# Moving the key weights by two 64-byte lines against the other matmul operands, with narrower warm-up matmuls

## The reference

```python
q = jnp.einsum('bchw,dc->bdhw', x, theta_w) + theta_b       # 256 channels, 1024 pixels
xpool = _maxpool2(x)                                        # 16 by 16 pixels
k = jnp.einsum('bchw,dc->bdhw', xpool, phi_w) + phi_b       # 256 by 256
v = jnp.einsum('bchw,dc->bdhw', xpool, g_w) + g_b           # 256 by 256
p = jax.nn.softmax(jnp.einsum('bdn,bdm->bnm', q, k) * hp ** (-0.5), axis=-1)
vp = jnp.einsum('bdm,bnm->bdn', v, p)
out = jnp.einsum('bdhw,cd->bchw', vp, z_w) + z_b + x
```

## The kernel before

| class | function | stationary | moving | matmuls |
|---|---|---|---|---|
| queries | `project_q` | `theta` | `x_split` | 96 a half |
| keys | `project_k` | `phi` | `xp` | 48 an image |
| values | `project_v` | `xp` | `g` | 48 an image |
| scores | `scores` | `q` | `k` | 24 a half |
| attention | `attend` | `vt` | `pt` | 24 a half |
| output | `project_out` | `z` | `att` | 84 a half |

## Time and profile before

### The profile page before, as it was taken

How to read it: one execution, slowest core, us unless ns; L and a number is a source line. 1 busy time by engine, 2 the same in 40 slices (tenths; PEclk the granted TensorE clock), 3 DMA queues, 4 the chain that set the end, 5 groups by cost and what they waited for, 6 DMA issues and landing times.

```text
span 2040.4 us, 48999 instructions
## 1 busy us (share of the span) xinstructions
PE 2026.8 (99%) x17790; PEld 2024.5 (99%) x17790; DVE 1558.1 (76%) x2625; ACT 1300.0 (64%) x2228; POOL 1366.5 (67%) x828
## 2 busy tenths in 40 slices
PE   9999999999999999999999999999999999999998
PEld 9999999999999999999999999999999999999998
DVE  8878777787777877777877778777787777787777
ACT  6666666666566665666666666666666566666663
POOL 4577666776666766667766677666677666776663
PEclk9999999999999999999999999999999999999999
DMA  7565656746556565566565664656656556656554
GB/s 243 191 212 184 213 169 214 236 170 210 175 207 232 180 210 185 186 226 210 181 212 171 215 237 169 209 177 207 232 180 210 184 187 226 209 182 214 170 193 166
DMA packets 213963, 407.27 MB, mean 200 GB/s; under 512 B 12720, under 2 KB 17840, under 8 KB 213936
## 3 DMA queue, kind: packets, MB, share of 16 engines
q1 hardware_dynamic: 213792, 406.90, 59.0%
q10 hardware_dynamic: 144, 0.01, 0.0%
HBM read 272.64 MB, written 134.22 MB: 199 GB/s over the span
## 4 chain that ended last, share of the span: by engine, by line
PE 97%; DVE 2%; POOL 0%; DMA 0%; issue 0%; ACT 0%; SPq 0%; DVEq 0%; POOLq 0%
PE bank L967 97%; DVE x_top L755 0%; DVE pt_raw L736 0%; DMA x<-x 0%; DVE x_bot L755 0%; DVE pooled L708 0%; POOL att_lo L631 0%; POOL x_split_lo L613 0%; POOL att_f L626 0%; DVE x L755 0%; PE bank L974 0%; SPq L265 0%; DVE q_lo L714 0%; ACT att_hi L425 0%; DVE xp_lo L851 0%
## 5 line engine op out<-in xcount | busy, mean ns | idle before, releaser
L613 POOL TENSOR_TENSOR x_split_lo<-x,x_split_hi 128x1024 fp32r<-128x1024 f32 x255 | 614.6, 2417 | 248.4 <-ACT x_split_hi L386 226.7
L967 PE MATMUL bank<-x_split_hi,theta_hi 128*128 128x256 f32 x2048 | 565.8, 276 | 3.1 <-POOL x_split_lo L613 2.0
L967 PE MATMUL bank<-x_split_lo,theta_hi 128*128 128x256 f32 x2048 | 565.7, 276 | 0.0
L967 PE MATMUL bank<-x_split_hi,theta_lo 128*128 128x256 f32 x2048 | 565.7, 276 | 0.0
L967 PE MATMUL bank<-att_hi,z_hi 128*128 128x256 f32 x1792 | 495.4, 276 | 3.6 <-DVE x_bot L755 2.5
L967 PE MATMUL bank<-att_hi,z_lo 128*128 128x256 f32 x1792 | 494.9, 276 | 0.0
L967 PE MATMUL bank<-att_lo,z_hi 128*128 128x256 f32 x1792 | 494.9, 276 | 0.0
L736 DVE STREAM_TRANSPOSE pt_raw<-probs 32x256 f32<-32x256 f32 x1024 | 445.9, 435 | 18.4 <-ACT probs L489 1.8
L631 POOL TENSOR_TENSOR att_lo<-att_f,att_hi 128x768 fp32r<-128x768 f32 x191 | 282.6, 1487 | 159.4 <-ACT att_hi L425 159.4
L967 PEld LDWEIGHTS bank<-x_split_hi,theta_hi 128*128 128x128 f32 x2048 | 384.6, 188 | 3.5 <-issue 3.5
L967 PEld LDWEIGHTS bank<-x_split_hi,theta_lo 128*128 128x128 f32 x2048 | 384.6, 188 | 0.0
(11 more groups left out here) (76 smaller groups left out, 4390.0 us busy)
## 6 DMA issues: line engine op xcount, KB each, us to landing
x<-x SPq DMA_DIRECT2D x258, 512.0 KB, 3.9
x_top<-x SPq DMA_DIRECT2D x128, 512.0 KB, 7.0
out<-x_top SPq DMA_DIRECT2D x128, 512.0 KB, 3.3
x_bot<-x SPq DMA_DIRECT2D x126, 512.0 KB, 5.2
out<-x_bot SPq DMA_DIRECT2D x126, 512.0 KB, 6.6
x_top<-theta_wt SPq DMA_DIRECT2D x4, 256.0 KB, 5.4
x_top<-g_wt SPq DMA_DIRECT2D x4, 256.0 KB, 5.4
x_bot<-z_wt SPq DMA_DIRECT2D x4, 256.0 KB, 6.2
```

The source lines that it names most:

```text
L613: nc.gpsimd.tensor_tensor(flat(lo), flat(x_chunk(s, c)), raw(flat(hi)), ALU.subtract).then_inc(x_ready, 1)
L967: last = nc.tensor.matmul(dst, stationary(a), moving(b), start=start and n == 0, stop=stop and n == len(PRODUCTS) - 1, skip_group_check=re ...
```

## The change

The pad ahead of `att` is gone and the pad ahead of `phi` is 48 words, not 16. All operands except `phi` move down by 64 bytes; `phi` and the float32 tiles behind it move up by 64 bytes. So the operand pairs of five classes keep their distance, moving minus stationary: line 3 minus line 0 before, line 2 minus line 7 after, which is 192 bytes modulo 512 both times. For the keys (`xp` moving, `phi` stationary) it was line 0 minus line 1, 448 bytes modulo 512, and is line 7 minus line 2, 320 bytes. The warm-up tile has 160 columns, not 192, and the four stretches have 62, 29, 17 and 43 matmuls, not 52, 24, 14 and 36.

```diff
-STILL = 192
+STILL = 160
@@
-        sb("pad_a", [P, 16], f32)
         att = [sb(f"att_{s}", [P, 7, HB], f32r) for s in ("hi", "lo")]
@@
         xp = [sb(f"xp_{s}", [P, KT, M], f32r) for s in ("hi", "lo")]
-        sb("pad_c", [P, 16], f32)
+        sb("pad_c", [P, 48], f32)
         phi = [sb(f"phi_{s}", [P, KT, D], f32r) for s in ("hi", "lo")]
@@
             pe.wait_ge(still_ready, 1)
-            keep_busy(o_x[1], 52)
+            keep_busy(o_x[1], 62)
@@
             project_q(0, 1, 1)
-            keep_busy(o_x[1], 24)
+            keep_busy(o_x[1], 29)
@@
                 pe.wait_ge(exp_done, upto(turn, s, NT, NT))
-                keep_busy(o_y[0], 36)
+                keep_busy(o_y[0], 43)
@@
                         pe.wait_ge(o_added, upto(turn, s - 1, SUMS, 2 * C11 + 2))
-                        keep_busy(o_y[1], 14)
+                        keep_busy(o_y[1], 17)
```

## The result

The changed kernel takes 2074.07 us (median of 4 runs, 2072.24 to 2075.73), the kernel before 2044.0 beside it: the ratio is 1.0148 [1.0136, 1.0160], 30 us slower. The forecast was 2043.6, with a range of 2034 to 2051; the measured time lies 23 us above that range.

A forecast was written before the change was run, and what follows sets the result against it. PE was taken as the bound, time being number of matmuls times distance between starts. Terms 0 + 0.03 + 0 on a 2040.4 us span, with the median 3.2 us above it, gave 2043.6 us, range 2034 to 2051.

The forecast's parts named there:

- What bounds the kernel: Whole run: PE busy 99% of 2040.4 us, nothing feeds it late; time is number of matmuls times distance between starts.
- the slow distance: Between matmul starts on PE: 117.7 ns against 113.3 ns fast; a stretch keeps the distance at which it started.
- the first term of the sum: Queries, scores, values, attention and output: 15324 matmuls keep 192 bytes modulo 512 between operands, so 0 us.
- The keys' own term: Keys' matmuls, operand difference 448 to 320 bytes: stay at 117.7 ns, no change, between ends of -7.3 and +6.6 us.
- The second rival: Keys leave the attention slow, so all 15324 other matmuls cost 4.4 ns more: +67 us, 2111, or 2104 with fast keys; chance 0.15.
- The first rival: Keys run fast and the rest too: -7.3 us, 2036.3, or 2034.3 with the first image fast as well; chance 0.33.
- handed on: At the first attention matmul behind the keys: attention takes over slow running, +67 us; chance 0.15.
- The third rival: Keys' matmuls get a longer distance, up to 122.1 ns: up to 2050 us; chance 0.10, of which 0.08 beyond the bound.
- The place of `phi` does nothing: Key weights' address has no effect, by the skill's rule of two independent read ports: 2043.6 us, counted with the forecast.
- Five other classes: All classes but keys: moving by one line to other absolute places is no reason for a cost, 0 us.
- Warm-up: Four warm-up stretches with narrower, more numerous matmuls: +0.03 us by columns, +0.65 us as the other end.
- Start, POOL: First image's and last step's starting distance: nothing, between -2.0 and +0.2 us; POOL's float32 tiles on another line: nothing.

## Why the prediction was wrong

**What bounds the kernel** was right: PE is the bound, nothing feeds it late, and the time is number times distance. The bound of the slow distance was right as well, 4.4 ns a matmul (117.8 - 113.4).

**The step that failed** is the first term of the sum, "I cost 15324 matmuls (16764 less 30 times 48 keys) at nothing". In 15 images the 504 matmuls behind the keys ran slow, and that cost 33.6 us. The keys' own term, "I take 117.7, no change", measured -3.2 us. Both rested on "The reason is the first image: ... whoever comes from another pair into it, or out of it, falls out of step". With the keys' pair (0, 3) in place of (0, 1), a fast output leads to fast keys (5.44 us at 1930.93), which it didn't before, and fast keys lead to a slow attention, with no wait behind it in the loop to end it.

**The second rival** had the mechanism, and the run that moves `phi` alone shows it to be the cause. Its price was wrong, 2104 with fast keys, because of "since all passes are alike". They aren't: in the loop, how the keys leave depends on how they came in. Fast keys leave slow, slow keys leave fast, slow output leads to slow keys and fast output to fast keys, and so every second image is slow: 30 us, not 60.

**The chance** was wrong by a row that stood in the forecast. The one case before in which keys ran fast, the first image, is followed by slow queries. The first rival, 0.33 for fast keys with the rest fast, needed a step from fast keys into a fast stretch, which no row shows and no run has shown since: wherever keys on line 0 ran fast and a class with its moving operand on line 3 followed directly, that class was slow. Keys fast should have carried "handed on" with it.

**The third rival**, up to 122 ns in the keys, didn't come at this place; at others the keys have 119.8 and 118.8.

**The place of `phi` does nothing**: it does, by 1.4%. The rule of the Trainium skill, "TensorE: Matmul & The Clock Gate", "Part 2: What happens when you issue a matmul", of two independent read ports, isn't enough to tell the time of a matmul here: with instructions and order alike, only an address has moved. The 188 and 192 ns that the forecast set against this rule don't differ by stretch: both rows are loads of the keys, 192 for one load in three.

**Five other classes**: that their own move by one line costs nothing was right by the run with `phi` alone (2073.28 against 2074.07). That the measure is bytes modulo 512 was a guess of the front part's table, and the run with line 5 agrees with modulo 256.

**Warm-up**: +0.03 us with +0.65 as the other end. Alone it gave +3 us (0.6 to 4.9), so by that run the end was too near, though nothing of it lies in the loop of its profile. Two other pairs of kernels with the narrow and the wide warm-up lie closer: the changed kernel and the one with `phi` alone, 30.1 and 29.3 us above before; `vt` on line 2 and on line 6, 3.3 and 3.8 us below. So the size isn't settled, nor where it arises.

**Start, POOL**: 1.6 us more ahead of the chain, 0.4 behind it, in one profile each; POOL's busy time went from 1366.5 to 1363.7 us. Neither changes the picture. Two small slips of the forecast's sums (31 x 0.24 is 7.4, not 7.3; 4.4 ns x 1488 is 6.5 us, not 6.6) don't either.

What stays open is why a step keeps or turns the distance. I had a theory of it, moments of a 6.67 ns beat at which the moving operand's line lets a matmul start; it missed with `xp` on line 3, with `phi` on line 0, with the added warm-up matmul and, by the attention, with `vt` on line 2, and the last two expectations rest on steps seen before, not on it. Neither the beat nor the five cycles that an expectation gave a step are shown by any run. The steps themselves are shown, in every image of the loop in which they occur but for one case (moving line, stationary line, modulo four; a dash where none occurs):

| step | coming in fast | coming in slow |
|---|---|---|
| output (3, 0) to keys (0, 1) | slow | slow (once, with `phi` on line 5) |
| output (3, 0) to keys (0, 3) | fast | slow |
| keys (0, 1) to attention (3, 0) | - (to queries slow, in the first image) | fast |
| keys (0, 3) to attention (3, 0) | slow | fast |
| keys (0, 0) or (0, 2), 119 to 120 ns, to attention (3, 0) | - | fast |
| keys (0, 3) to attention (3, 2) | slow | - |
| attention (3, 2) to scores (3, 0) | fast | fast (slow once, behind a warm-up) |
| attention (3, 0) to scores (3, 2) | fast | slow |
| scores (3, 2) to values (3, 0) | - (to queries fast) | fast |
| between equal pairs (3, 0) | fast | slow |

The case that departs from the table is in the profile with `vt` on line 6. Its attention behind the warm-up, from 86.49 us on, is slow, and the scores behind it are slow as well (2.83 us), so that one image is slow. These are the first matmuls of scores and values:

```profile
89.40 0.28 PE L967 MATMUL bank<-k_hi,q_hi 128*128 128x256 f32 x1
...
92.23 0.28 PE L967 MATMUL bank<-g_hi,xp_hi 128*128 128x256 f32 x1
```

Ahead of the loop there is a second such case. Slow keys with the pair (0, 3) that start behind the first image's warm-up lead to slow queries in the run with `phi` alone (24 in 2.82 us, from 35.97) and to fast queries in the changed kernel (2.73 us, from 37.71). So whether a stretch is fast or slow doesn't always tell what it hands on; what else it carries behind a warm-up stays open.

## What to carry to other kernels

Where one engine runs without a break, its time is count times distance, and the distance can have more than one value for the same instruction: read it class by class from start times, and look at two neighbouring periods before calling all of them alike. An inefficient stretch may be what puts the rest back into step, so before removing it ask what state it hands on, and find the row that shows the state after the efficient one. Here, padding that puts one stationary operand two 64-byte lines off its neighbours gave such a return for 24 slow matmuls an image.

## What the runs showed of the hardware

Matmuls of one shape (128 by 128 weights loaded for each, 256 columns, fp32r) start 113.3, 117.8 or 119.8 ns apart (5.44 us / 48, 59.37 us / 504 and 5.75 us / 48), and 118.8 with the keys' operands two lines apart, at the same granted clock (0.998 to 1.000 over each execution), by the 64-byte lines of their operands and by the step into the stretch. Places 256 bytes apart ran alike in the two cases tried, `phi` on lines 1 and 5 and `vt` on lines 2 and 6. A stretch of hundreds of matmuls doesn't find back from the slow distance to the fast one by itself: in the changed kernel 504 slow matmuls in a row, over five classes, kept it to their end, 59.37 us. With `phi` on lines 0, 1, 2 and 3 the medians are 2045.2, 2043.6, 2046.6 (with the narrow warm-up) and 2073.3 us: in the loop the keys are fast only on line 3, and there the kernel is slowest. The cost of placement alone, from the best kernel to the worst without an added instruction, is 73.6 us in 2039.8, 3.6%.
